# A state-space layer and a routed expert layer on one core: third matrices loaded later in four pieces, part of the last sum on VectorE, a third gate buffer, all orders remade

## What is computed

```python
# layer 1, a state-space layer with 256 inner channels and 16 states
xn = layernorm(x) * w + b
x_in, z = split(xn @ in_proj_w.T)
x_act = silu(conv1d(x_in, taps=4) + conv_b)
delta_s, B, C = split(x_act @ x_proj_w.T)          # 1, 16, 16 columns
delta = softplus(delta_s @ dt_w.T + dt_b)
h[t] = h[t-1] * exp(-delta[t]) + B[t] * x_act[t]   # per channel and state
y[t] = sum_s h[t] * C[t]
out = (y * silu(z)) @ out_proj_w.T + x
# layer 2, 16 experts, the two best of each token, 512 hidden features
w, idx = top2(softmax(x @ Wr + br)), normalised
out = sum over the token's 2 experts e of
      w_e * layernorm((silu(x @ W1[e]) * (x @ W3[e])) @ W2[e]) * gamma[e] + beta[e]
```

## Time and profile before

| | |
|---|---|
| runs, median | 1057.6 us (1056.78 to 1058.89, 3 runs) |
| profiled execution | 1051.54 us |
| its span, first to last instruction | 1049.0 us |
| busy in the span: TensorE, VectorE, ScalarE, GpSimd | 923.4, 731.4, 722.3, 647.5 us |
| mean granted clock of TensorE | 0.952 of full speed |
| moved by DMA | 75.20 MB |

### The profile page before, as it was taken

One profiled execution on the slowest core, in us unless ns is written; L12 is line 12 of the kernel. 1 busy time (PEld: TensorE's weight loads), 2 busy tenths in 40 slices (PEclk: granted clock), 3 DMA queues, 4 the chain that ended last, 5 costly groups with the idle time before them and its releaser, 6 DMA issues.

```text
span 1049.0 us, 25919 instructions
## 1 busy us (share of the span) xinstructions
PE 923.4 (88%) x6855; PEld 786.0 (75%) x6855; DVE 731.4 (70%) x2451; ACT 722.3 (69%) x1422; POOL 647.5 (62%) x827
## 2 busy tenths in 40 slices
PE   5899999999999999999852599999999999999783
PEld 2666767667767667776651599999999999999731
DVE  1277788887888988778864267677777777777654
ACT  3567876778777777767542477777777877777535
POOL 1324576766667776666755366666666666566648
PEclk9899999999999999999875699999999999999987
DMA  8000110111110111110157531111111111111093
GB/s 285 12 11 31 47 41 24 44 52 47 48 32 29 51 51 37 36 33 21 42 181 313 171 103 48 49 47 53 46 50 48 46 51 46 48 49 47 16 349 131
DMA packets 52188, 75.20 MB, mean 72 GB/s; under 512 B 11055, under 2 KB 32817, under 8 KB 51280
## 3 DMA queue, kind: packets, MB, share of 16 engines
q1 hardware_dynamic: 40816, 54.87, 16.2%
q0 software_dynamic: 8672, 16.93, 4.5%
q10 hardware_dynamic: 2560, 1.75, 0.6%
HBM read 47.09 MB, written 27.41 MB: 71 GB/s over the span
## 4 chain that ended last, share of the span: by engine, by line
PE 55%; DVE 16%; issue 11%; POOL 9%; ACT 6%; DMA 3%; POOLq 0%; DVEq 0%; SPq 0%; ACTq 0%
PE pA L1675 10%; PE pR L1675 10%; PE pB L1683 5%; PE pY L1683 5%; PE pY L1533 4%; PE pA L1419 4%; PE pB L1445 3%; DVE placed L1240 2%; POOL chosen_scratch L635 2%; ACT xb L686 2%; PE pR L1561 2%; DMA xin<-in_x_dram 2%; DVE Hs L1076 2%; PE pR L1517 2%; DVE y_both L1115 2%
## 5 line engine op out<-in xcount | busy, mean ns | idle before, releaser
L635 POOL DMA_INDIRECT chosen_scratch<-yo,got_id x143 | 147.9, 1034 | 94.3 <-issue 88.4
L944 ACT ACTIVATE stage<-w_sb 128x1024 f32 x143 | 151.2, 1057 | 51.9 <-issue 37.6
L592 POOL DMA_INDIRECT slots_scratch<-xrow,send_at x128 | 139.6, 1091 | 39.8 <-issue 36.8
L1324 DVE TENSOR_TENSOR hidT<-pR,sil 128x512 f32<-128x512 f32 x143 | 98.9, 692 | 85.5 <-ACT sil L939 61.6
L1675 PE MATMUL pA<-xsT,stage 128*128 128x128 f32 x1144 | 152.8, 277 | 0.4 <-ACT xsT L928 0.4
L1675 PE MATMUL pR<-xsT,stage 128*128 128x128 f32 x1144 | 152.0, 277 | 0.0
L1675 PEld LDWEIGHTS pA<-xsT,stage 128*128 128x128 f32 x1144 | 140.8, 194 | 0.7 <-ACT xsT L928 0.7
L1675 PEld LDWEIGHTS pR<-xsT,stage 128*128 128x128 f32 x1144 | 139.9, 193 | 0.0
L1419 PE MATMUL pA<-xn,taps 128*128 128x512 f32 x256 | 129.4, 610 | 1.0 <-DVE taps L976 1.0
L625 POOL TENSOR_TENSOR ers<-eve,neg_half 128x1 f32<-128x1 f32 x143 | 81.2, 568 | 51.5 <-DVE eve L1336 49.4
L939 ACT ACTIVATE sil<-pA 128x512 f32<-128x512 f32 x143 | 85.2, 596 | 27.1 <-PE pA L1675 25.3
(11 more groups left out here) (187 smaller groups left out, 2137.9 us busy)
## 6 DMA issues: line engine op xcount, KB each, us to landing
got<-slots_scratch SPq DMA_DIRECT2D x143, 65.0 KB, 1.8
w_sb<-chosen_scratch SPq DMA_DIRECT2D x16, 512.0 KB, 5.2
w_sb<-in_w_dram SPq DMA_DIRECT2D x1, 6144.0 KB, 17.8
xin<-in_x_dram SPq DMA_DIRECT2D x16, 256.0 KB, 2.8
xr<-in_x_dram SPq DMA_DIRECT2D x16, 256.0 KB, 2.9
w_sb<-in_w_dram SPq DMA_DIRECT2D x1, 4096.0 KB, 14.6
x_scratch<-x SPq DMA_DIRECT2D x16, 256.0 KB, 3.2
fx<-x_scratch SPq DMA_DIRECT2D x1, 4096.0 KB
```

The lines of the kernel that those rows point to most:

```text
L592: eng.indirect_dma_start(slots_d, bass.IndirectOffsetOnAxis(ap=send_at[:, s % 2, k, t:t + 1], axis=0), xrow[:, s % 2, k, t, :], None).then ...
L635: eng.indirect_dma_start(chosen_d, bass.IndirectOffsetOnAxis(ap=got_id[:, j % NGOT:j % NGOT + 1], axis=0), yo[:, q, :], None, bounds_check ...
L944: eng.activation(stage[:, j % NSTAGE, :, :].rearrange("p k f -> p (k f)"), w13_sb[:, bass.ds(e, 1), :, :].rearrange("p o k f -> p (o k f)" ...
L1324: eng.tensor_tensor(hidT[:, p, :], pR[:, p, :], sil[:, p, :], ALU.mult).then_inc(hid_ready, 1)
```

## The change

It does seven things.

1. `w2_sb` is loaded in four transfers of four experts each, behind `store_x1` of sequences 1 to 4 instead of ahead of `load_x(2)`. In the drain, `store_x1(14)` goes ahead of `load_xr(15)` and `load_early`.
2. `gate_w` counts on `w_loaded`, like the other small weights.
3. `zs` has three buffers; `gate_z` waits for the sequence three before.
4. `dec2`, `dec4`, `dec8` have two buffers; the `join` steps wait for `fold` of the sequence two before.
5. In the last sum VectorE adds the first group of each pair (1, 3, ..., 13; semaphore `f_o_dve`), GpSimd the others.
6. The pair sum of group 0 is an add on VectorE from SBUF to SBUF instead of TensorE's product.
7. The orders of `unit` on GpSimd, ScalarE, VectorE and TensorE are new. Three steps pass the border of a round, with their `q` moved by one: `scan` (VectorE), `r_half(., 2)` (ScalarE), and `bc_turn(., 1)`, `diag_turn` and `project_gate(., 0)` (TensorE).

```diff
+DVE_ADDS = tuple(range(1, 15, 2))
+POOL_ADDS = tuple(g for g in range(16) if g not in DVE_ADDS)
...
-        sum_bank = lambda g: (pA, pB, pR, pY)[g % 8 // 2][:, g % 2, :]
+        sum_bank = lambda g: w13_sb[:, 0, 0, :] if g == 0 else (pA, pB, pR, pY)[g % 8 // 2][:, g % 2, :]
...
+            def load_w2(q):
+                eng.dma_start(w2_sb[:, :, 4 * q:4 * q + 4, :], w2[:, :, 4 * q:4 * q + 4, :]).then_inc(w2_loaded, 16)
...
-            eng.dma_start(w2_sb[:, :, :, :], w2).then_inc(w2_loaded, 16)
             load_x(2)
...
             store_x1(1)
+            load_w2(0)
             load_x(7)
...
# GpSimd, unit
                 join(q[3], 2)
+                address(q[5])
                 carry(q[3], 4)
                 join(q[3], 4)
+                join(q[3], 8)
                 carry(q[3], 8)
-                join(q[3], 8)
-                address(q[5])
+                rstd_1(q[0])
                 rstd_3(q[4])
+                residual(q[4])
                 token(q[4])
-                rstd_1(q[0])
-                residual(q[4])
                 rstd_4(q[4])
# ScalarE, unit
-                rt_copy(q[4], 2)
+                r_half(q[4], 2)
                 conv_out(q[3], 0)
                 gate_z(q[3], 0)
+                rt_copy(q[4], 2)
...
-                yh_copy(q[4], 4)
                 rt16_copy(q[4], 0)
                 rt16_copy(q[4], 1)
                 yh_copy(q[4], 8)
                 block_decay(q[4], 0)
+                yh_copy(q[4], 4)
                 block_decay(q[4], 1)
                 x1_norm(q[5])
                 ht_copy(q[4], 0)
+                weights(q[6])
                 ht_copy(q[4], 1)
-                weights(q[6])
...
                 xf_norm(q[5])
+                xs_copy(q[3])
                 xf_twice(q[5])
-                xs_copy(q[3])
                 r_odd(q[3])
+                decay(q[3])
                 xft_copy(q[5])
-                decay(q[3])
# VectorE, unit
-                scan(q[4], 0)
-                scan(q[4], 1)
                 stats_4(q[5])
                 aggr_4(q[5])
-                shift_1(q[1])
+                stats_1(q[0])
                 var_4(q[5])
-                stats_1(q[0])
                 fold(q[4], 8)
...
                 expand(q[3], 0)
-                dots(q[3])
                 gather(q[4], 1)
                 expand(q[3], 1)
                 decayed(q[4])
+                dots(q[3])
+                with_diagonal(q[4])
                 logits(q[5])
                 largest(q[5])
-                with_diagonal(q[4])
+                margin(q[5])
                 where(q[5])
                 choose(q[5])
                 gated(q[4])
                 positions(q[5])
-                mask(q[3], 2)
+                mask(q[3], 4)
                 diagonal(q[3])
                 odd(q[3])
-                mask(q[3], 4)
-                aggr_1(q[0])
+                mask(q[3], 2)
                 attend(q[4])
                 stats_3(q[4])
+                aggr_3(q[4])
+                aggr_1(q[0])
+                var_3(q[4])
                 var_1(q[0])
-                aggr_3(q[4])
-                var_3(q[4])
                 shift_3(q[4])
-                margin(q[5])
+                shift_1(q[0])
+                scan(q[3], 0)
+                scan(q[3], 1)
# TensorE, unit
-                r_turn(q[4], 2)
+                bc_turn(q[4], 1)
+                diag_turn(q[4])
+                project_gate(q[3], 0)
+                odd_turn(q[4])
                 gram(q[4], 4)
                 gram(q[4], 2)
                 rank(q[6])
+                r_turn(q[4], 2)
                 project_gate(q[3], 1)
-                odd_turn(q[4])
                 project_out(q[5])
...
                 conv(q[2], 0, 1)
+                delta_turn(q[3])
+                conv(q[2], 0, 2)
+                bc_turn(q[3], 0)
                 xf_turn(q[5])
                 next_b(q[3])
-                delta_turn(q[3])
-                conv(q[2], 0, 2)
+                conv(q[2], 0, 3)
                 route(q[5])
-                bc_turn(q[3], 0)
-                diag_turn(q[3])
-                bc_turn(q[3], 1)
-                conv(q[2], 0, 3)
-                project_gate(q[2], 0)
...
# VectorE, last sum
+            def last_add(h):
+                g = PARTS[h][0]
+                eng.wait_ge(f_n, g + 1)
+                eng.tensor_tensor(fx1[:, g, :, :], fn[:, h % 2, 0, :, :], fx1[:, g, :, :], ALU.add).then_inc(f_o_dve, 1)
+
+            eng.wait_ge(fx1_loaded, 16)
+            eng.wait_ge(f_loaded[0], 16)
+            eng.tensor_tensor(w13_sb[:, 0, 0, :], w13_sb[:, 0, 0, :], w13_sb[:, 0, 1, :], ALU.add).then_inc(f_o_dve, 1)
             for h in range(len(PARTS)):
                 last_stats(h)
                 last_aggr(h)
                 last_var(h)
+                if h >= 2:
+                    last_add(h - 1)
```

More of the change, by code:

```diff
@@ L164, in sandwich @@
         u = sb("u", [P, 2, 2, SEQ])
-        zs = sb("zs", [P, 2, 2, SEQ])
+        zs = sb("zs", [P, 3, 2, SEQ])
         dec1 = sb("dec1", [P, 2, 2, SEQ])
-        dec2 = sb("dec2", [P, 2, SEQ // 2])
-        dec4 = sb("dec4", [P, 2, SEQ // 4])
-        dec8 = sb("dec8", [P, 2, SEQ // 8])
+        dec2 = sb("dec2", [P, 2, 2, SEQ // 2])
+        dec4 = sb("dec4", [P, 2, 2, SEQ // 4])
+        dec8 = sb("dec8", [P, 2, 2, SEQ // 8])
         dec16 = sb("dec16", [P, 2, SEQ // 16])
@@ L387, in _ @@
                 eng.dma_start(dst, src).then_inc(first_loaded, 16)
[L388 removed]
+            eng.dma_start(gate_w[:, :], in_wT).then_inc(w_loaded, 16)
             load_x(1)
@@ L440, in _ @@
             store_x1(13)
+            store_x1(14)
             load_xr(15)
             load_early()
-            store_x1(14)
             load_late()
@@ L516, in decs @@
             def decs(s, h):
-                return {1: dec1[:, s % 2, :, :], 2: dec2[:, :, :], 4: dec4[:, :, :], 8: dec8[:, :, :], 16: dec16[:, :, :]}[h]
+                return {1: dec1[:, s % 2, :, :], 2: dec2[:, s % 2, :, :], 4: dec4[:, s % 2, :, :], 8: dec8[:, s % 2, :, :], 16: dec16[:, :, :]}[h]
             def pairs(t):
@@ L657, in last_add @@
             def last_add(h):
-                for q in range(PARTS[h][1]):
-                    g = PARTS[h][0] + q
-                    eng.wait_ge(f_n, g + 1)
-                    eng.tensor_tensor(fx1[:, g, :, :], fn[:, h % 2, q, :, :], fx1[:, g, :, :], ALU.add).then_inc(f_o, 1)
+                q = PARTS[h][1] - 1
+                g = PARTS[h][0] + q
+                eng.wait_ge(f_n, g + 1)
+                eng.tensor_tensor(fx1[:, g, :, :], fn[:, h % 2, q, :, :], fx1[:, g, :, :], ALU.add).then_inc(f_o, 1)
             eng.wait_ge(fx1_loaded, 16)
@@ L909, in unit @@
                 bct_copy(q[3], 1)
-                r_half(q[3], 2)
             run_units(NS, NS + DEPTH, unit)
@@ L1083, in first_decay @@
             def first_decay(s, h):
-                d = {1: dec1[:, s % 2, :, :], 2: dec2[:, :, :], 4: dec4[:, :, :], 8: dec8[:, :, :]}[h]
+                d = {1: dec1[:, s % 2, :, :], 2: dec2[:, s % 2, :, :], 4: dec4[:, s % 2, :, :], 8: dec8[:, s % 2, :, :]}[h]
                 return d.rearrange("p m (b k) -> p (m b) k", k=2)[:, :, 0:1].broadcast_to([P, SEQ // h, h])
@@ L1365, in last_stats @@
                 for q in range(PARTS[h][1]):
-                    eng.wait_ge(f_sum, PARTS[h][0] + q + 1)
+                    if h == 0:
+                        eng.wait_ge(f_o_dve, 1)
+                    else:
+                        eng.wait_ge(f_sum, PARTS[h][0] + q)
                     for t in range(NT4):
@@ L1704, in pair_sum @@
                 i.then_inc(f_sum, 1)
-            for g in range(NG):
+            for g in range(1, NG):
                 pair_sum(g)
```

37 lines of the change are left out of this document (23 added, 14 removed).

## The result

| | before | after |
|---|---|---|
| median of the runs | 1057.19 us (4 runs, 1054.27 to 1058.89) | 1040.10 us (4 runs, 1039.45 to 1041.66) |
| ratio, 95% interval | | 0.9841 [0.9818, 0.9863] |
| profiled execution, its span | 1051.54, 1049.0 | 1040.41, 1038.6 |

The change makes the kernel 1.6% faster.

The account below looks back on a forecast made before the run. In the rounds no engine is full; a loop over engines sets their length. Terms -0.8 - 5.5 + 0.1 - 6.3 = -12.5 gave 1039.0 for the profiled execution and a 1045.1 us median; range 1033 to 1053.

Parts of the forecast that it names:

- fill: Start up to the first state scan: third matrices in pieces free x(2) and keep TensorE's clock up, -5.5 us.
- The 0.6 that I gave to the orders: Start: `delta_turn` ahead of `next_b` and a shorter way from `carry(1)` to the scan, -0.6 us.
- Rounds: Pipelined rounds: gain on `with_diagonal` taken again by `carry(1)` and `margin`; 15 x -0.05 = -0.8 us, bounds -3 and +6.
- `margin`: Rounds, VectorE: moved in front of `where`, it meets `carry(1)` at the port and ends near 292.0, `join(1)` near 293.0.
- Drain: After the last sequence's scan: `margin` now precedes the last routing, +0.1 us; `store_x1(14)` going first, nothing.
- Last sum: End of kernel: sharing adds makes TensorE the bound at 3.43 per pair; -6.3 us, bounds -1.5 and -7.5.
- rival 2: Last sum: stays at 4.1 per pair because VectorE's and GpSimd's operations wait for each other; 1050 us, chance 0.13.
- offset: Whole kernel: median of runs shown, 1057.6, is 6.1 above the profiled execution, turning 1039.0 into 1045.1.
- expert tiles: Stretch from 588.45 to 995.34 us, between the tables and the last sum: left alone by the change.
- Rival 1: Rounds: `placed` gets the port before `carry(2)`, some 1.5 us per round, 13 rounds, -20; 1025 us, chance 0.10.
- Rival 3: Start: gives 1 instead of 5.5 us, as the scan waits for something else or the clock falls anyway; 1050, chance 0.15.
- Rival 4: Rounds: a later moment chain (`residual`, `stats_4`, `stats_1`, `var_4`) holds up `fold`; 1.5 more gives +15, 1060 us; chance 0.09.

Follow-up runs that it names:

- `positions` cut in two: Kernel after with `mask` of level 4 and `diagonal` ahead of `placed` and `pos`, while `place` and `running` stay ahead: 1016.64 us, ratio 0.9664, period 30.20.
- the plain move: Kernel after with VectorE's `mask` of level 4 and `diagonal` ahead of all of `positions`, and GpSimd's `address` behind `carry(8)`: 1030.49 us, ratio 0.9808, period 31.14.

## Why the prediction was right, and where its terms were not

- **Direction and mechanism of the fill: right.** -5.5 was forecast, -6.5 came (first scan near 49 forecast, 48.23 measured), with no stretch of the lower clock at 34 to 40 and no wait for x(2). The 6.5 are 2.8 up to `conv_out`, 2.4 more up to `carry(1)`, and 1.3 from there to the scan. Alone the transfer gives 6.7 in the profile and 5.9 in the times, where I had 4.9 for it. The 0.6 that I gave to the orders is neither shown nor refuted: they take 0.4 off the first scan without the pieces (55.46 against 55.82) and 0.7 with them (48.38 against 49.09), but the kernel before alone has its first scan at 54.75 in one profile and 55.82 in another. In the second one TensorE's clock is at 0.59 already from 30 to 34 us, where the first has 0.98, and `project_state` takes 3.59 instead of 2.69.
- **Rounds: mechanism right, size wrong.** -0.05 per round was forecast, -0.20 came, and -1.14 in the first round, which I had not looked at; -3.5 instead of -0.8. `with_diagonal` first, 1.2 long, `carry(1)` stretched to over 2, `placed` unmoved: all as forecast, and `with_diagonal` starts 8.55 behind `fold`, where I had counted 8.54. That match is luck: I took 0.75 off for `logits`, `largest` and a gap, and the kernel with that move alone has 8.74, so they are worth 0.56, and the other 0.19 goes with `dots`, which I had not counted. The term that was off is `margin`: I let it use the port between `carry(1)` and `join(1)`, which put `join(1)` 0.15 later. It ends with `carry(1)` (283.01 against 282.99) and `join(1)` starts at 282.95. The kernel with `margin` elsewhere has the same period, which shows that it costs nothing. Three readings of mine were off without harm. `join(1)` ended 0.90 behind `with_diagonal` (293.03 and 292.13), not 0.98. It is not only operations with two inputs in SBUF that are stopped: the cast has one, and so has `fve` in the last sum. And VectorE also waited for GpSimd once a round (1.16 at 303.90), just ahead of its wait of 2.29 for TensorE.
- **Drain: off in the first profile, within the scatter otherwise.** +0.1 was forecast, the first profile has +4.86, the second profile of the same kernel 59.70, against 59.44 and 60.90 in two profiles of the kernel before. The growth is one chip's or one execution's, and with 1.5 between two profiles of one kernel a term of 0.1 can't be tested.
- **Last sum: mechanism right, bound wrong.** -6.3 was forecast and -5.6 came. I had TensorE as the new bound and the last add ending at 1039.3 in the times of before, 43.96 behind the store; it ends 45.04 behind it (1035.57 - 990.53). TensorE itself ends as counted (35.48 behind the store, 35.9 by my count); the last add comes 9.56 behind it, not 8.1. That is the part of rival 2 that came true: in every second pair VectorE's add and GpSimd's power meet and the power is 0.4 longer, and in the pairs between GpSimd's add makes `fve` 0.4 longer, which makes 3.68 per pair, not 3.43 and not 4.1. The Trainium skill (SBUF — State Buffer, Who interferes with whom) has the rule that the one of the two engines that comes second is blocked for the whole instruction of the other. By that rule, the trace agrees where the add is first, to within 0.14: the power at 1020.22 starts 0.14 into an add of 0.69, would have to wait 0.55, and is 0.41 longer. Where the power is first, the trace does not agree: VectorE's add at 1024.12 starts 0.17 into the power of 1023.95, which lasts 1.64, and takes 0.69 all the same. The measurement decides: that order costs nothing here, and why is not shown.
- **The sum is 4.6 short, and the offset is not why.** I added 6.1 for the distance of the median of before to its profiled execution, so that -12.5 gave 1045.1; 1040.1 was measured. But medians of one series say -17.1 and -17.2, where I had -12.5, so the missing part is in the terms. The profiles of both kernels on one chip (spans 1049.8 and 1032.7) say in which: fill -7.4 (forecast -5.5), rounds -3.3 (-0.8), drain -1.2 (+0.1), expert tiles +0.3 (0), last sum -5.5 (-6.3), together -17.1. The rounds are the worst of them, by a factor of four, then the fill. Against the first profile of the kernel after my 1039.0 looks better than it is (1040.41): its slow drain, +4.86, covers what the rounds and the fill gave beyond the forecast. That is luck.
- **Where the 6 us between runs and profile come from.** On the later chips the kernel before takes 1051.4 to 1052.6, and the kernel after 1034.2: 4.6 to 5.9 less than on the first. So the first runs of both carry some 5 us that the profiled execution of before, by its 1051.54, seems not to carry, while that of the kernel after (1040.41) does. Its profile shows where: 4.6 of its 5.9 are behind the last scan, in a wait of 2.67 and in blank stores at 1.6 to 1.7 instead of 1.0 to 1.1 us each. What slows the stores there stays open: they were slow in one profile only, and the same kernel had them quick in the next. Whether the runs without a profile had them slow too is not shown.
- **Rivals.** Rival 1 (`placed` gets past `carry(2)`) did not happen. Taking `placed` off the path by another way gave 1.44 per round where I had 1.5, but only with `positions` cut in two; the plain move gave 0.50. What stops `placed` is not fully read: its row starts 0.59 ahead of `carry(2)` and its own work is 0.28, so it is the first of the two already, and still it ends last. A send runs in those 0.59 us, but the last `placed` of the kernel after, at 562.03, also starts within a send and takes 0.29. No run shows what holds it. Rival 2 came true in part, as said. Rival 3 falls by the kernel with the pieces alone. Rival 4, the moment chain, did not decide: ScalarE's queue ties that chain to TensorE's, and it did not hold `fold` up, which waits 0.74 for ScalarE's `y_first`.

## What to carry to other kernels

When two engines exclude each other in a row of operations, the time of the last of them follows here from when the first starts (3.5 to 3.6 us in three orders): moving one within the row, or taking a stretched one out, moved nothing. What paid was to take the operation that nobody on the path needs (`placed`) out of the path altogether; and then look at once for what it releases besides its result, since two thirds of the gain (0.94 of 1.44 us per round) hung on a bank that a small operation beside it still read.

Compare medians of the same chip and series, and take the terms of a sum from profiles of the same chip. Here the two first profiles said 11.1 us and the medians beside them 17.1; the medians were the ones that came again.

## What had not been expected

- The same kernel differs by 5 to 6 us from chip to chip or series to series (before: 1057.2 and 1052.6; after: 1040.1 and 1034.2), while the runs of one series lie within 5.2 us, and the two ratios are 0.9841 and 0.9842.
- A store of 65 KB took 1.01 to 1.10 us in thirteen profiles and 1.6 to 1.7 in one (eight of them in 12.65 and 13.61).
- A VectorE operation on 128x4 elements took 0.65 us, and the cast of 128x8 elements 0.30, 0.38 or 0.84, each ending within 0.04 of a GpSimd operation on 128x512.
